# Third layer's conditioning path between the pairs of the first attention

## The reference

```python
cc = silu(c)
h = bitlinear(cc, wa0, na0)                     # 128 -> 128
y = bitlinear(h, wa1, na1)                      # 128 -> 2 x 576
gate, y = split(y, 2)
h = bitlinear(silu(gate) * y, wa2, na2)         # 576 -> 128
h = bitlinear(h, wa3, na3, ba3)                 # 128 -> 768
h = rmsnorm(h, wr, 1e-6)
params = bitlinear(h, wa4, na4, ba4)            # 768 -> 768

def bitlinear(x, w, nw, b=None):
    xn = x * rsqrt(mean(x * x) + 1e-8) * nw
    s = 127 / clip(max(abs(xn)), 1e-5)
    xq = clip(round(xn * s), -128, 127) / s
    wq = clip(round(w / mean(abs(w))), -1, 1) * mean(abs(w))
    return xq @ wq.T (+ b)
```

## Time and profile before

| | |
|---|---|
| median of 3 runs | 516.98 us (511.12 to 519.7) |
| the profiled execution | 518.54 us, of it 516.7 us from the first to the last instruction |
| PE busy | 392.2 us (76%) |
| DVE busy | 332.2 us (64%) |
| ACT busy | 272.5 us (53%) |
| POOL busy | 136.4 us (26%) |
| mean clock granted to PE | 0.837 of full |

### The profile page before, as it was taken

The page is one execution under the profiler, slowest core; times in us unless marked ns, Lnnn a source line. Parts: engine busy times, 40 slices in busy tenths (PEclk is TensorE's granted clock), DMA queues, the critical chain, the costliest instruction groups (busy, mean ns, idle before and its releaser), DMA issues.

```text
span 516.7 us, 7343 instructions
## 1 busy us (share of the span) xinstructions
PE 392.2 (76%) x2488; PEld 253.2 (49%) x2489; DVE 332.2 (64%) x815; ACT 272.5 (53%) x748; POOL 136.4 (26%) x162
## 2 busy tenths in 40 slices
PE   4989999989999979669898889889971521246564
PEld 4656567557567655445465445445541411104343
DVE  4447888646777843795847656512299189789784
ACT  1475554698697534365474452554424840475342
POOL 1043343433455620102306310001012032280101
PEclk9999999999999998988759858996995555555597
DMA  8950000000000000000000000000000000000001
GB/s 313 437 202 1 1 1 1 1 2 2 0 2 1 1 2 1 0 1 1 1 0 1 2 1 1 1 1 1 1 0 0 1 1 0 1 1 0 1 0 41
DMA packets 3836, 13.26 MB, mean 26 GB/s; under 512 B 372, under 2 KB 2420, under 8 KB 3284
## 3 DMA queue, kind: packets, MB, share of 16 engines
q1 hardware_dynamic: 3800, 12.80, 6.2%
HBM read 12.28 MB, written 0.52 MB: 25 GB/s over the span
## 4 chain that ended last, share of the span: by engine, by line
PE 58%; DVE 24%; ACT 7%; issue 7%; POOL 2%; DMA 1%; POOLq 0%; SPq 0%; ACTq 0%; DVEq 0%
PE bank L955 7%; PE bank L935 6%; PE bank L982 6%; PE bank L969 6%; PE bank L940 3%; DVE area L1428 3%; PE bank L1053 3%; PE bank L1001 3%; DVE tab_ L1428 3%; DVE area L1431 3%; PE bank L1208 2%; PE bank L1187 2%; DVE nmax L1575 2%; PE bank L1106 2%; PE bank L1282 2%
## 5 line engine op out<-in xcount | busy, mean ns | idle before, releaser
L532 ACT ACTIVATE big<-bank 128x512 f32<-128x512 f32 (+1 forms) x104 | 53.2, 532 | 64.7 <-PE bank L1192 44.2
L532 ACT ACTIVATE area<-bank 128x512 f32<-128x512 f32 (+3 forms) x68 | 37.2, 552 | 53.4 <-PE bank L940 16.4
L1575 DVE TENSOR_REDUCE nmax<-bank 128x2 f32<-128x512 f32 x64 | 42.4, 681 | 32.1 <-PE bank L1165 31.9
L456 POOL TENSOR_TENSOR big<-big,rrec 128x512 f32<-128x512 f32 x44 | 44.9, 1041 | 67.8 <-DVE rrec L1630 67.7
L1614 DVE TENSOR_REDUCE nmax<-bank 128x2 f32<-128x512 f32 x64 | 43.4, 680 | 29.3 <-PE bank L955 29.2
L1622 DVE COPY area<-bank 128x512 f32<-128x512 f32 x64 | 42.6, 684 | 9.4 <-PE bank L969 8.6
L532 ACT ACTIVATE big<-bank,nmax 128x256 f32<-128x256 f32 x88 | 41.1, 479 | 12.1 <-PE bank L935 8.1
L935 PE MATMUL bank<-xT,w0s 128*128 128x256 f32 x128 | 33.9, 396 | 5.5 <-issue 5.4
L955 PE MATMUL bank<-area 64*128 64x256 f32 x256 | 36.3, 402 | 0.0
L982 PE MATMUL bank<-area 128*64 128x256 f32 x256 | 34.7, 391 | 0.6 <-ACT big L532 0.6
L1297 PE MATMUL bank<-identb,area 128*128 128x128 bf16 x40 | 6.0, 309 | 38.1 <-DVE area L1431 38.0
(11 more groups left out here) (237 smaller groups left out, 885.5 us busy)
## 6 DMA issues: line engine op xcount, KB each, us to landing
w2s<-w SPq DMA_DIRECT2D x1, 4352.0 KB, 26.2
rows<-row SPq DMA_DIRECT2D x1, 1600.0 KB, 10.9
w0s<-w SPq DMA_DIRECT2D x3, 512.0 KB, 6.8
w1s<-w SPq DMA_DIRECT2D x1, 1408.0 KB, 15.7
w0s<-w SPq DMA_DIRECT2D x1, 1024.0 KB, 12.9
xs<-x SPq DMA_DIRECT2D x1, 512.0 KB, 4.1
out<-tab_ SPq DMA_DIRECT2D x2, 256.0 KB, 2.3
tabs<-tab SPq DMA_DIRECT2D x1, 423.5 KB, 5.1
```

The costliest lines, as they stand in the source:

```text
L456: pool.tensor_tensor(prob[n % SLOTS], prob[n % SLOTS], rrec0[:, n % 4, :].unsqueeze(2).to_broadcast([P, QT, SEQ]), ALU.mult).then_inc(S("a ...
L532: return nc.scalar.activation(o, i, f, **kw)
L1575: V.tensor_reduce(nmax[:, c % 2, :, h % 8], ring_bank("S", n, 0)[:, :].rearrange("p (q k) -> p q k", q=QT), AX, ALU.max, negate=True).then ...
```

## The change

The path leaves the second attention and goes into the first. Each step of the first attention gets three places, z = 3s, 3s+1 and 3s+2, on ACT (`ada`: sums of squares and the exponential of the gate), DVE (`ada`: rows, takes, results, gate) and PE (`ada`: turns and products, at the first and the third place); POOL takes the deviations between two pairs. On DVE the first place stands behind the reciprocal, the second behind the first copy of a pair, the third behind the second copy. `BEGIN` and `USE` give the places: the path begins in step 12 and its last instructions stand in step 34.

- PE: all `kept_busy` products of the path are left out; those of rounds 0 to 10 and of `turn_values` stay. Turns go to bank 5, products to banks 4 and 5, the banks of the probabilities' turns, which then wait for the path's copies (`ada_read`).
- DVE copies the products out instead of ACT, for `wa3` and `wa4` with their bias in the same instruction.
- The gate is exp(-g) on ACT, then on DVE plus one, reciprocal, times g and times the other half. The Silu of `c` moves to the start of ACT's program, behind a wait for the transfer of the path's rows, and this transfer moves on SP's queue from the last place to the place before the query weights.
- The rows lie in places that are free in the first attention (the used modulation weights, the spent half of the weights of `wa1`, the row tile); a gap of zeros in the row tile makes room.
- The second attention's ring holds scores, maxima, values and outputs alone.
- POOL quantises the six matrices of the recurrence in one piece, once the first maxima of the second attention have been taken.

```diff
+        BEGIN = {"wa0": 37, "wa1": 47, "wa2": 63, "wa3": 74, "wr": 85, "wa4": 88}
+        USE = {"wa0": 40, "wa1": 49, "wa2": 67, "wa3": 76, "wr": 88, "wa4": 91}
+        TOP, WORTH, SCALE, CLIP, TURN, TAKE, PRODUCT = 1, 2, 3, 4, 5, 6, 7
+        GATE = USE["wa1"] + PRODUCT + 2
+        PARAMS = USE["wa4"] + PRODUCT + 4
...
             sp.dma_start(tabs[:, :], tab).then_inc(S("tab_in"), 16)
+            sp.dma_start(adrs[:, :], adr).then_inc(S("adr_in"), 16)
...
             for p in range(PAIRS):
                 normalised(p)
                 if p % 8 == 2 and p > 8:
                     batch_rstd(p // 8 - 1)
+                for name, z in BEGIN.items():
+                    if z // 3 - 1 == p:
+                        ada_deviation(name)
...
-            for c, (name, width) in enumerate(ADA_DEVIATIONS.items()):
...
-                for which in BEHIND.get(name, ()):
-                    whole_weights(which)
+            pool.wait_ge(S("a1_M"), 1)
+            for name in ("wi", "wf", "wg", "wo", "wm1", "wm2"):
+                whole_weights(name)
...
+            act.wait_ge(S("adr_in"), 16)
+            acti(SRC["wa0"], SRC["wa0"], ACT.Silu).then_inc(S("silu_row"), 1)
...
+                for name in ("wa1", "wa3"):
+                    if z == BEGIN[name]:
+                        act.wait_ge(S("ada_piece"), ada_pieces(name))
+                        ada_square(name)
+                if z == GATE:
+                    act.wait_ge(S("ada_piece"), ada_pieces("wa1") + 2)
+                    acti(forget4, gate4, ACT.Exp, scale=-1.0).then_inc(S("ada_exp"), 1)
...
+                if ada_read[n % 2]:
+                    pe.wait_ge(*ada_read[n % 2])
...
+            def ada_turned(name, s):
+                n, r = ADA_SHAPE[name][0:2]
+                pe.wait_ge(S("ada_row"), 3 * ADA_NAMES.index(name) + 3)
+                pe.wait_ge(S("a0_pT"), min(2 * s - 4, 2 * PAIRS))
+                for ch in range(n):
+                    m = nc.tensor.transpose(bank[5][0:r, ch * 4:ch * 4 + 4], line4[:, ch * r:(ch + 1) * r],
+                                            ident[0:NB, 0:NB])
...
+                pe.wait_ge(S("a0_pT"), min(2 * s - (4 if ada_bank(k) == 5 else 3), 2 * PAIRS))
...
-                kept_busy(TURN_BUSY[name], to[:, 256:512])
...
-                    to = turn_maxima((i - M_LAG) // 8)
-                    if i == WEAVE["wa2"] + 1:
-                        kept_busy(24, to[:, 256:512])
+                    turn_maxima((i - M_LAG) // 8)
...
-                weave(i)
-                weave(i + 1)
...
+            def ada_use(name):
+                dve.wait_ge(S("ada_rstd"), list(ADA_DEVIATIONS).index(name) + 1)
...
+                V.scalar_tensor_tensor(o, SRC[name], a4s[:, 2:3], by, ALU.mult, ALU.mult).then_inc(S("ada_row"), 1)
...
+            def ada_gate(z):
+                if z == GATE + 2:
+                    dve.wait_ge(S("ada_exp"), 1)
+                    gates_made[0] = mark(ts(forget4, forget4, 1.0, None, ALU.add))
...
                 prepared(s, 0)
+                ada(3 * s + 0)
...
                 if turned_pair is not None:
                     take0(2 * turned_pair)
                 prepared(s, 1)
+                ada(3 * s + 1)
...
                 prepared(s, 2)
+                ada(3 * s + 2)
```

More of the change, by code:

```diff
@@ L298, in ada_weight, with splits, ada_products, ada_results @@
             return t[:, start:start + hi - lo]
[L300 to L310 removed]
+        ADA_PIECE = {"wa0": P, "wa1": 384, "wa2": P, "wa3": 384, "wa4": 384}
+        def splits(name):
+            width, piece = ADA_SHAPE[name][2], ADA_PIECE[name]
+            return [(lo, min(lo + piece, width)) for lo in range(0, width, piece)]
+        BEGIN = {"wa0": 37, "wa1": 47, "wa2": 63, "wa3": 74, "wr": 85, "wa4": 88}
[3 more added lines that the diff above has]
+        PARAMS = USE["wa4"] + PRODUCT + 4
+        def ada_products(z):
+            return [(name, k) for name in ADA_NAMES for k in range(len(splits(name)))
+                    if z == USE[name] + PRODUCT + (0, 1, 3)[k]]
+        def ada_results(z):
+            return [(name, k) for name in ADA_NAMES for k in range(len(splits(name)))
+                    if z == USE[name] + PRODUCT + (0, 2, 3)[k]]
+        def ada_bank(k):
+            return 5 if k == 1 else 4
         NH = NB * H
@@ L394, in parts_of, with by_piece @@
             return t.bitcast(dt) if dt is not F32 else t
-        SRC = {"wa0": part(adrs, ADR, "c"), "wa1": a4[:, 2, 0:P], "wa2": a4[:, 0, 0:ADA], "wa3": a4[:, 2, 0:P],
-               "wr": a4[:, 0, 0:OUT6], "wa4": a4[:, 2, 0:OUT6]}
-        DST = {"wa0": a4[:, 2, :], "wa1": a4[:, 2, :], "wa2": a4[:, 2, :], "wa3": a4[:, 0, :], "wa4": params}
+        def by_piece(v):
+            return v.rearrange("p (a n) -> p a n", n=192)
+        line4 = w0s[0:NB, 0:OUT6]
+        rough = xn[0:NB, 7, :]
+        gate4 = w2s[0:NB, W2["wa1"][0]:W2["wa1"][0] + 2 * ADA].rearrange("p (a n) -> p a n", a=3)[:, :, 192:384]
+        forget4 = by_piece(adrs[:, 0:ADA])
+        up4 = by_piece(line4[:, 0:ADA])
+        bias3 = part(adrs, ADR, "ba3")
+        SRC = {"wa0": part(adrs, ADR, "c"), "wa1": rough, "wa2": gate4, "wa3": rough, "wr": bias3, "wa4": bias3}
         def m1_bank(u):
@@ L617, in _ @@
                     rounds(u)
+                ada(3 * s)
                 for i in units[1:2]:
@@ new lines, in ada_result @@
+            def ada_result(name, k):
+                lo, hi = splits(name)[k]
+                src = bank[ada_bank(k)][0:NB, 0:hi - lo]
+                dve.wait_ge(S("ada_mm"), ada_pieces(name) + k + 1)
+                if name in ("wa3", "wa4"):
+                    m = V.scalar_tensor_tensor((bias3 if name == "wa3" else params)[:, lo:hi], src, a4s[:, 5:6],
+                                               part(adrs, ADR, "ba" + name[2], lo, hi), ALU.mult, ALU.add)
+                elif name != "wa1":
+                    m = ts(rough, src, a4s[:, 5:6], None, ALU.mult)
+                elif k == 0:
+                    m = ts(gate4[:, 0:2, :], by_piece(src), a4s[:, 5:6], None, ALU.mult)
+                elif k == 1:
+                    ts(gate4[:, 2, :], src[:, 0:192], a4s[:, 5:6], None, ALU.mult)
+                    m = ts(up4[:, 0, :], src[:, 192:384], a4s[:, 5:6], None, ALU.mult)
+                else:
+                    m = ts(up4[:, 1:3, :], by_piece(src), a4s[:, 5:6], None, ALU.mult)
+                m.then_inc(S("ada_piece"), 1)
```

260 lines of the change are left out of this document (121 added, 139 removed).

## The result

The changed kernel takes 512.1 us (median of 20 runs, 509.6 to 518.3), the kernel before 516.7 (20 runs, 511.1 to 519.7): a ratio of 0.9938, 95% interval 0.9913 to 0.9964. That is faster by 0.6%, inside what I had called no change, and a third of the 1.9% forecast. The profiled executions have spans of 510.8 and 516.7 us. The 5.9 us between them are what is left of two much larger terms and two small ones, and both large terms of the prediction were off, in opposite directions. The marks are starts in TensorE's time lines: the first product of scores, the first turn of the second layer norm (L912 before, L930 after), the first scores of the second attention, the shifted scores of round 64, the end.

A forecast was written before the change was run, and what follows sets the result against it. TensorE was taken as full in the first attention's last batch and busiest in the second, at a reduced clock. -21.6 + 12.1 = -9.5 us took the profiled 518.54 to 509.0, and the median, 1.56 lower, to 507 us; range 497 to 517.

The forecast's parts named there:

- both large terms of the prediction: 21.6 us saved in the second attention up to round 64, and 12.1 us added in the first attention.
- What enters the first attention: The conditioning path's work placed in the first attention's steps adds 12.1 us, bounds 5 and 18.
- VectorE's overload: First attention, steps 24 to 31: 7.9 us of row work against some 0.5 free per step, 4.1 us over.
- Port waits: First attention, steps 24 to 31: five VectorE instructions each wait 0.65 us on GpSimd's normalisation, 3.2 us.
- What leaves the second attention: Fill products, row products, small turns and TensorE's waits on rows go: 21.6 us saved, 18 to 26.
- pieces: Second attention savings: to round 12 1.8 us, 12 to 18 2.3, 18 to 34 2.1, 34 to 50 9.7, 50 to 64 5.7.
- the pace: Second attention: a double round takes 1.65 to 1.70 us at the upper clock and 2.57 at the lower.
- Behind round 64 nothing changes: From round 64 of the second attention to the end: 0 us of change.
- the rows holding up the pairs: Rival, first attention: whole-normalisation port waits and late squares holding GpSimd and the next turn, 18 us added, 513 us; 15%.
- The clock did fall: Judges the rival that the second attention's clock doesn't fall: rounds 18 to 34 take 16.6 us, 497 us in all; 8%.
- did come back: Judges the rival that `turn_values` of round 34 no longer raises the second attention's clock: 528 us; 5%.
- Rows are swallowed: Rival: the first attention's copies and maxima run far enough ahead, only TensorE's own 5 us remain, 500 us; 20%.

The follow-up runs named there:

- Late turns: Changed kernel with turns two places later, separate banks, a tanh gate and the last row's turn and products in the second attention: 501.2 us, ratio 0.9659.
- own banks: Changed kernel with the last three rows' turns and second product pieces in bank 7 instead of bank 5: 506.2 us, ratio 0.9803.
- the tanh: Changed kernel with the gate by a tanh on ScalarE instead of an exponential and reciprocal: 508.8 us, ratio 0.9890.
- the last row's late turn: Changed kernel with turn, products and results of `wa4` moved into rounds 2 to 9 of the second attention: 509.8 us, ratio 0.9874.
- the third place: Kernel with late turns, own banks and the tanh, with first use and scaling of four rows one place later on VectorE: 499.5 us, ratio 0.9588.
- the fill: Changed kernel with three more 128x512 fill products in each of rounds 12, 14 and 16 of the second attention: 510.4 us, ratio 0.9874.

## Why the prediction was off

**What enters the first attention: the step that failed.** I gave TensorE its own turns and products, 4.3 us in all, and charged the rest to the rows, VectorE's overload above all: 12.1 us, at most 18. Measured: 30.5. The rows alone cost 12.0, and turns and products at the upper clock, added up from the time line, some 6. What I left out is that TensorE stops at every hand-over with VectorE. The diff shows these waits (`ada_read` before a turn, `ada_row` and `a0_pT` in `ada_turned`), and I priced none: 15.0 us of waits, and behind three of them the lower clock, 1.6 and 1.3 us at two output products and some 3 at 199 to 206 us. These overlap with what the rows cost: with turns, products and their waits taken out and the rows kept, the stage is 18.5 us shorter. I had asked who waits for VectorE's late steps only of the pairs' maxima and copies, not of the path's own. Late turns, own banks, the tanh and the last row's late turn together bring the added time from 30.5 to 10.9 us.

The sum also went wrong by place. I forecast 1.8 us in steps 12 to 23, 8.1 in steps 24 to 31 and 1.5 behind (and 0.7 for GpSimd anywhere); the three parts above, the last with step 31 in it, grew by 7.5, 10.9 and 12.1. VectorE got 26.3 us of work in the stage (busy 97.0 against 70.7 us), and I had priced 7.9, all of it in steps 24 to 31. In the first part alone it got 12.7, for which I put nothing and gave no reason. That the rows alone came to 12.0 all the same, near the 12.1 of the whole sum, is luck.

**The reciprocal** was in the diff and not in my list. Its price could be had from the kernel before: reciprocals of 4, 32 and 64 elements a partition take 169, 353 and 553 ns there, 6.3 to 6.6 ns an element, so 576 make 3.7 us. Measured 3.73; the stage without it is 4.9 us shorter, of which the clock may be a part.

**Port waits.** The mechanism was right and the stretch well sized. Use and scaling of the fourth and last row and the use of `wr` took 1.17, 0.54, 1.83, 2.28 and 0.88 us, 3.5 more than the prices that I had set beside them (0.34, 0.27, 1.0, 1.0, 0.60); I had 3.2. As time of the stage such a stretch counted by half in steps 24 to 31 and by nothing before, as the third place shows (1.7 us taken away for 0.9, and 2.0 for nothing) in the kernel with late turns.

**What leaves the second attention.** Places and order of the clock's moves came as forecast; the term was 29.6 us, beyond its upper bound of 26. By pieces, forecast and measured: 1.8 and 1.7; 2.3 and 3.1; 2.1 and 4.5; 9.7 and 12.7; 5.7 and 7.7. The mis-sized number is the pace: I took 1.65 to 1.70 and 2.57 us, by single double rounds of the earlier trace rows that looked free (1.69 and 2.59), where the stage without the path runs at 1.48 and 2.30, and 1.2 us for a rest of the low stretch that wasn't there. I had kept 1.5 for the bound, as a little more than two maxima on VectorE take. The value was right, but the reason isn't borne out: TensorE is the busiest engine there, 10.70 of 11.24 us, ahead of VectorE's 9.30. So that was luck. The cover counted too: the 88 fill products, which I had listed first among what was saved, were worth nothing by themselves.

**"Behind round 64 nothing changes"** holds for the work and not for the time: 5.1 us, all clock (in the kernel before it was at the lower level from 352 to 362 us, in the changed one not). A further 1.9 us came between the attentions; no run singles out their cause.

**The rivals.** The time came nearest to the rows holding up the pairs (513 us, 15%), but not by its mechanism, port waits and late squares. The clock did fall and did come back, so those two are out. Rows are swallowed only in part, even in the best version. That the whole came within some 5 us of the forecast is luck too: the first attention missed by 18.4 us one way, and the other three terms by 15.0 the other.

## What to carry to other kernels

When work moves into a pipeline of two engines, list for each new instruction which hand-over it adds and how far behind the other engine then is, not only how long it takes: TensorE stopped for 15 us at turns and banks while the work itself was 6. Place a consumer a whole step behind its producer and give it a bank that nobody else is waiting for: here the path then cost a third in this stage, with the reciprocal gone and the last row's turn moved out as well. Price every engine's share in every stretch, also where the engine looks idle. And read the pace of a stage from the work of its busiest engine in a round (TensorE's, 1.48 us), not from the best round of a disturbed trace.

## What was not expected of the hardware

- In the changed kernel's first attention the granted clock fell to the lower level at waits of 0.9 to 3.4 us, but the same wait was followed by a fall in one execution and not in another (1.92 us: a fall at 127 us in the changed kernel, none with the fill). Behind round 64 nothing tells an execution with a fall from one without: the same rows ended at 1.00 in one kernel and at 0.61 in another. The Trainium skill (TensorE: Matmul & The Clock Gate, section Why this matters for your kernels) puts drops down to idle gaps between bursts; the traces agree in part: the falls in the first attention came at gaps, though not every gap of that size brought one, and filling the longer gap ahead of round 64's fall (0.91 us) didn't avert it.
- Nine fill products in the thin rounds 12 to 16 kept the clock up there: 8.9 us off the second attention.
- Fill products had a price of less than nothing where rows are awaited: 88 taken out, 6.5 us lost, in one execution.
- A small vector step that reads two rows is not cheap beside GpSimd: 4x128 took 0.33 us in one place and 1.17 to 2.00 in others.
